# A graph network on one core: the adjacency build's last two column blocks kept as the first layers' ring, and the head's small stages rearranged

## The reference

```python
s = concatenate([src, arange(n)]); d = concatenate([dst, arange(n)]); w = concatenate([edge_weight, ones(n)])
deg = segment_sum(w, d, n); dinv = where(deg > 0, rsqrt(deg), 0.0)
norm = dinv[s] * w * dinv[d]
h = x @ W                                        # once for each layer
out = segment_sum(h[s] * norm[:, None], d, n) + b
```

## Time and profile before

| | us |
|---|---|
| median of three runs | 3757.71 |
| the profiled execution, its time | 3750.24 |
| its span, first to last instruction | 3748.5 |
| search, to the first memset of the build | 50.3 |
| build, to the first load of the degrees | 50.3 to 287.2 |
| degrees, to the first memset of the pair tables | 287.2 to 319.6 |
| pair tables, to the load of x | 319.6 to 354.0 |
| node rows, to the first product of the layers | 354.0 to 377.5 |
| first layers, to the load of the next activation table | 377.5 to 800.3 |

### The profile page before, as it was taken

The page is one execution under the profiler, slowest core; times in us unless marked ns, Lnnn a source line. Parts: engine busy times, 40 slices in busy tenths (PEclk is TensorE's granted clock), DMA queues, the critical chain, the costliest instruction groups (busy, mean ns, idle before and its releaser), DMA issues. The chain is left out here.

```text
span 3748.5 us, 47928 instructions
## 1 busy us (share of the span) xinstructions
PE 3235.0 (86%) x13936; PEld 2084.9 (56%) x13936; DVE 1413.7 (38%) x3323; ACT 1300.0 (35%) x2198; POOL 922.2 (25%) x927
## 2 busy tenths in 40 slices
PE   5872999975999996388888869999999999999994
PEld 3661555544888884277667645555555555555541
DVE  6992100023666665488888840010000000000003
ACT  1440000021555554277777732222222222222223
POOL 2000000005777770077777700000000000000000
PEclk9995999995776776699999979999999999999997
DMA  1443676723333330166566547667667676676740
GB/s 40 187 187 131 289 300 285 302 100 75 77 82 78 82 77 7 55 181 166 161 165 169 158 155 294 281 277 296 277 285 290 272 300 277 278 300 269 292 185 17
DMA packets 172645, 721.48 MB, mean 192 GB/s; under 512 B 43149, under 2 KB 139151, under 8 KB 159724
## 3 DMA queue, kind: packets, MB, share of 16 engines
q1 hardware_dynamic: 128802, 631.24, 42.7%
q0 software_dynamic: 33920, 84.12, 9.2%
q10 hardware_dynamic: 9681, 3.07, 0.3%
HBM read 669.95 MB, written 48.38 MB: 192 GB/s over the span
## 5 line engine op out<-in xcount | busy, mean ns | idle before, releaser
L900 PE MATMUL deep_out_psum<-deep_adjacency,deep_scaled_nodes 125*128 125x450 f32 (+1 forms) x3500 | 1334.6, 537 | 0.0
L900 PEld LDWEIGHTS deep_out_psum<-deep_adjacency,deep_scaled_nodes 125*128 125x128 f32 x3500 | 656.9, 189 | 625.0 <-issue 625.0
L1629 POOL DMA_INDIRECT gate_source_rows_sb<-gate_source_rows,pair_src x416 | 454.0, 1091 | 293.7 <-POOLq L1066 167.2
L1235 POOL DMA_INDIRECT source_rows<-gat_source_rows,pair_src x416 | 420.0, 1010 | 126.8 <-issue 125.0
L900 PE MATMUL gcn_out_psum<-gcn_adjacency,gcn_scaled_nodes 125*128 125x450 f32 (+1 forms) x1050 | 399.1, 539 | 0.0
L1671 PE MATMUL gate_core_psum<-edge_weights,edge_features_t 128*128 128x256 f32 x832 | 263.7, 399 | 46.9 <-ACT edge_features_t L1705 45.5
L900 PEld LDWEIGHTS gcn_out_psum<-gcn_adjacency,gcn_scaled_nodes 125*128 125x128 f32 x1050 | 198.0, 190 | 188.9 <-issue 188.9
L923 ACT ACTIVATE deep_squares<-deep_aggregate,deep_vectors 128x450 f32<-128x450 f32 (+1 forms) x70 | 46.8, 668 | 629.4 <-DVE deep_aggregate L968 629.4
L973 DVE SCALAR_TENSOR_TENSOR deep_normed<-deep_aggregate,deep_vectors,deep_squares 128x450 f32<-128x450 f32 (+1 forms) x70 | 47.9, 685 | 565.5 <-ACT deep_squares L927 565.5
L442 PE MATMUL adjacency_sum<-weighted_cell,source_onehot 128*128 128x150 f32 x1042 | 177.6, 311 | 41.3 <-DVE weighted_cell L418 41.2
L1673 PE MATMUL gate_core_psum<-gate_target_rows,gate_node_onehot_t 125*128 x1248 | 208.5, 275 | 0.0
(11 more groups left out here) (359 smaller groups left out, 4210.5 us busy)
## 6 DMA issues: line engine op xcount, KB each, us to landing
deep_adjacency<-adjacency SPq DMA_DIRECT2D x70, 5625.0 KB, 16.2
gcn_adjacency<-adjacency SPq DMA_DIRECT2D x21, 5625.0 KB, 16.2
adjacency<-adjacency_columns SPq DMA_DIRECT2D x7, 5625.0 KB, 16.9
edge_features<-in_edge_attr_dram SPq DMA_DIRECT2D x416, 64.0 KB
att_node_rows<-pair_dst_rows SPq DMA_DIRECT2D x104, 125.0 KB
gate_node_rows<-pair_dst_rows SPq DMA_DIRECT2D x104, 125.0 KB
source_rows<-gat_source_rows,pair_src POOLq DMA_INDIRECT x416
gate_source_rows_sb<-gate_source_rows,pair_src POOLq DMA_INDIRECT x416
```

The lines of the kernel that those rows point to most:

```text
L900: m = nc.tensor.matmul(op[:, n % 2, 0:cols], h[:, l % 2, s, :], ring[0:T, n % 2, s, 0:cols], start=s == 0, stop=s == NS - 1)
L1235: pool.indirect_dma_start(xj[:, b % HOLD, q, :], None, d["h_r"], bass.IndirectOffsetOnAxis(ap=c["pair_src"][:, b * PQ + q:b * PQ + q + 1], ...
L1629: pool.indirect_dma_start(xj[:, b % 4, q, :], None, d["p_src"], bass.IndirectOffsetOnAxis(ap=c["pair_src"][:, b * PQ + q:b * PQ + q + 1], ...
```

## The change

The build visits the column blocks in the order 2, 3, 4, 5, 6, 0, 1, so blocks 0 and 1 are the last in the staging tile; this tile becomes the first layers' ring, and the layers' first two blocks are read where they were built. All seven blocks are still stored, for the later layers. The tile is allocated from the start, and the search stage uses it as work space.

The node rows are loaded (third in SP's queue) and turned during the search: 25 transposes by TensorE, between the product that finds the rows and the products of the sizes, with copies by ScalarE. The tables of extra blocks (two groups of products and five VectorE instructions) move from the search to the build, after units 6, 13, 14 and 21; block 0's extra passes wait for them. Five small VectorE instructions turn a place in the order into a group's number.

The degree parts go from the stage to 25 rows of SBUF, 25 products with ones sum them into a [125, 25] tile, which is already by nodes; one transpose and a copy give the rows that are stored and then broadcast. The stage waits for the store and no more for the broadcast; the layers' VectorE stream does. The layers' weights are loaded on ScalarE's queue in this stage.

The pair tables' steps stand between the layers' blocks: VectorE's after blocks 0, 2, 4, ... 12 (behind L968), TensorE's after blocks 1, 3, ... 11 (behind the block's last product), ScalarE's loads at the layers' start and its stores after blocks 9 and 11. The stages of pair tables and of node rows are gone, with one reset of the semaphores.

```diff
--- before.py
+++ after.py
...
-        "deg_rows": nc.dram_tensor("degree_part_rows", [NSP, NS, BW], F32).ap(),
...
+HELD = 2
+TURN = (NSP - HELD) * GB
+ORDER = [(b + HELD) % NSP for b in range(NSP)]
...
-def edge_lanes(nc, c, d, x_src, x_dst, x_w):
+def edge_lanes(nc, c, d, x_src, x_dst, x_w, x, columns):
...
+        spare = columns[:, 1, :, :].rearrange("p s c -> p (s c)")
+        el = spare[0:ER, 0:4 * EC].rearrange("p (c w) -> p c w", w=4)
+        xn = columns[0:T, 0, :, 0:D]
...
             sp.dma_start(ei[:, 1, :], x_dst.rearrange("(p c) -> p c", p=ER)).then_inc(s_ld, 16)
             sp.dma_start(ei[:, 0, :], x_src.rearrange("(p c) -> p c", p=ER)).then_inc(s_ls, 16)
+            sp.dma_start(xn, x.rearrange("(s r) f -> r s f", r=T)).then_inc(s_lx, 16)
...
+            for q in range(NXQ):
+                n = min(4, NS - 4 * q)
+                act.wait_ge(s_xt, q + 1)
+                nc.scalar.copy(c["x_t"][:, 4 * q * T:(4 * q + n) * T].rearrange("f (s r) -> f s r", r=T), p_t[:, q % GC, 0:n, 0:T]).then_inc(s_xc, 1)
...
+            pe.wait_ge(s_lx, 16)
+            for s in range(NS):
...
+                t = nc.tensor.transpose(p_t[:, s // 4 % GC, s % 4, 0:T], xn[:, s, :], c["ident"][0:T, 0:T])
...
             pe.wait_ge(s_mask, 1)
             pe.wait_ge(s_sr, 1)
...
-            pe.wait_ge(s_bc, 1)
-            for k in range(GC):
-                m = nc.tensor.matmul(p_g[:, 0:UO], c["ones"][:, :], begun[:, k, :], start=k == 0, stop=k == GC - 1)
-            m.then_inc(s_sp, 1)
-            for k in range(GC):
-                m = nc.tensor.matmul(p_n[0:1, 0:UO], dv[:, k:k + 1], begun[:, k, :], start=k == 0, stop=k == GC - 1)
-            m.then_inc(s_sp, 1)
+            pe.wait_ge(s_xc, NXQ)
...
+            o.link(vec.tensor_scalar(wraps[:, :], place[:, :], float(TURN), -float(NSP * GB), ALU.is_ge, ALU.mult))
+            o.link(vec.scalar_tensor_tensor(group[:, :], place[:, :], float(HELD * GB), wraps[:, :], ALU.add, ALU.add))
+            o.link(vec.tensor_scalar(own[:, 0, :], group[:, :], float(G), None, ALU.mult))
+            vec.tensor_scalar(own[:, 1, :], group[:, :], float(NS * G), None, ALU.mult)
+            o.link(vec.tensor_tensor(node[:, 0, :, :], node[:, 1, :, :], own[:, 0, :].unsqueeze(2).to_broadcast([128, GC, G]), ALU.add))
...
 def build_adjacency(nc, c, d, stage):
...
+        SPREAD_AT, PLACED_AT, FIRST_AT, LISTED_AT = 6, 13, 14, 21
...
+        slot = [(b + NSP - HELD) % 2 for b in range(NSP)]
...
+                if n == PLACED_AT:
+                    dve.wait_ge(s_xs, 1)
+                    vec.tensor_scalar(c["extra_cells"][:, :], xps[:, 0:UO], float(NS * G), float(NS * G * (HELD * GB - 1)), ALU.mult, ALU.add)
+                    vec.tensor_scalar(c["extra_column"][:, :], xps[0:1, 0:UO], float(G), float(G * (HELD * GB - 1)), ALU.mult, ALU.add).then_inc(s_xp, 1)
+                    vec.tensor_scalar(steps[:, :], c["ramp"][0:1, 0:UO], float(EL), float(EL), ALU.mult, ALU.add).then_inc(s_xv, 1)
+                if n == LISTED_AT:
+                    dve.wait_ge(s_xs, 2)
...
+                    vec.tensor_tensor(e0r[:, :], xps[0:1, 0:UO], steps[:, :], ALU.add).then_inc(s_xv, 1)
+                    dve.wait_ge(s_xv, 2)
+                    vec.tensor_scalar(c["extra_first"][:, :], e0r[:, :], float(E), None, ALU.min).then_inc(s_xl, 1)
...
+                if n == SPREAD_AT:
+                    for k in range(GC):
+                        i = nc.tensor.matmul(xps[:, 0:UO], c["group_steps"][:, k, :], c["group_begun"][:, k, :], start=k == 0, stop=k == GC - 1)
+                    i.then_inc(s_xs, 1)
+                if n == FIRST_AT:
+                    pe.wait_ge(s_xp, 1)
+                    for k in range(GC):
+                        i = nc.tensor.matmul(xps[0:1, 0:UO], c["extra_edge_step"][:, k:k + 1], c["group_begun"][:, k, :], start=k == 0, stop=k == GC - 1)
+                    i.then_inc(s_xs, 1)
...
-                sp.dma_start(d["deg_rows"][b:b + 1, :, :], stage[T:T + 1, b % 2, :, :]).then_inc(s_dg, 16)
-                sp.dma_start(d["adj"][b], stage[:, b % 2, :, :]).then_inc(s_st[b % 2], 16)
+                first = ORDER[b] * BW
+                sp.dma_start(c["degree_parts"][0:NS, first:first + BW], stage[T:T + 1, slot[b], :, :]).then_inc(s_dg, 16)
+                sp.dma_start(d["adj"][ORDER[b]], stage[:, slot[b], :, :]).then_inc(s_st[slot[b]], 16)
...
-def degrees(nc, c, d):
+def degrees(nc, c, d, ly):
...
+            for s in range(NS):
+                m = nc.tensor.matmul(p_d[:, s:s + 1], c["degree_parts"][0:NS, s * T:(s + 1) * T], c["ones"][0:NS, 0:1], start=True, stop=True)
+            m.then_inc(s_d, 1)
+            pe.wait_ge(s_n, 1)
+            nc.tensor.transpose(p_r[:, 0:T], c["dinv_n"][:, :], c["ident"][0:T, 0:T]).then_inc(s_t, 1)
...
-            for b in range(NSP):
-                act.dma_start(sums[b * BP:(b + 1) * BP, :, :], d["deg_rows"][b].rearrange("s (x j) -> x s j", j=DJ)).then_inc(s_ld, 16)
+            ly.begin(act, d)
...
+            nc.scalar.copy(c["dinv_rows"][:, :], p_r[:, 0:T]).then_inc(s_c, 1)
+            act.wait_ge(s_c, 1)
+            act.dma_start(d["dinv"].rearrange("(s r) -> s r", r=T), c["dinv_rows"][:, :]).then_inc(s_st, 16)
             act.wait_ge(s_st, 16)
...
-                act.dma_start(c["dinv_n"][:, :], d["dinv"].rearrange("(s r) -> r s", r=T)).then_inc(s_bk, 16)
-            act.dma_start(c["dinv_b"][:, :], d["dinv"].unsqueeze(0).to_broadcast([128, N])).then_inc(s_bk, 16)
-            act.wait_ge(s_bk, 32)
+            act.dma_start(c["dinv_b"][:, :], d["dinv"].unsqueeze(0).to_broadcast([128, N])).then_inc(c["dinv_loaded"], 16)
...
-def edge_path(nc, c, d, x_src, x_dst):
...
+class EdgePath:
...
+    def tensor(self, pe, n):
...
+        if n == 1:
+            pe.wait_ge(self.s_bl, 1)
             for t in range(UTL):
...
+        if n == 3:
+            pe.wait_ge(self.s_ps, 1)
+            nc.tensor.matmul(ps[:, 1, 0:KP], c["ones"][0:NS - 1, :], self.passed[:, :], start=True, stop=True).then_inc(self.s_gr, 1)
+        if n == 5:
+            pe.wait_ge(self.s_pk, 1)
             for t in range(UTL):
+                m = nc.tensor.matmul(ps[:, 2, 0:KP], self.dst_f[:, t, :], self.pick[:, t, :], start=t == 0, stop=t == UTL - 1)
...
+        if n == 7:
+            pe.wait_ge(self.s_dl, 2)
...
+        if n == 9:
+            pe.wait_ge(self.s_tc, 1)
+            pe.wait_ge(self.s_bm, 2)
...
+        if n == 11:
+            pe.wait_ge(self.s_bs, 1)
+            pe.wait_ge(self.s_ba, 8)
...
-def load_transposed(nc, c, tag, x, out, bias=None, then=None):
...
-        self.load(sp, d, 0)
-        self.load(sp, d, 1)
+        for n in range(self.held, 2):
+            self.load(eng, d, n)
...
-def gcn_layers(nc, c, d, ly):
+def gcn_layers(nc, c, d, ly, path=None):
...
+            if ly.held:
+                for k in range(2):
+                    sp.wait_ge(c["adj_stored"][k], 16 * len(range(1 - k, NSP, 2)))
             for n in range(2, len(blocks)):
                 sp.wait_ge(s_bs, n - 1)
                 ly.load(sp, d, n)
...
-                pe.wait_ge(ly.s_a[n % 2], (n // 2 + 1) * 16)
+                if n >= ly.held:
+                    pe.wait_ge(ly.s_a[n % 2], ((n - ly.held) // 2 + 1) * 16)
...
                 m.then_inc(s_bs, 1)
+                if path is not None:
+                    path.tensor(pe, n)
...
+            if ly.held:
+                dve.wait_ge(c["dinv_loaded"], 16)
...
                 vec.tensor_tensor(yk, op[:, n % 2, 0:cols], c["dinv_b"][:, c0:c0 + cols], ALU.mult).then_inc(s_br, 1)
+                if path is not None:
+                    path.vector(dve, n)
...
-        edge_path(nc, c, d, a["src"], a["dst"])
-    c["sems"].end()
...
+        gcn_layers(nc, c, d, ly, EdgePath(nc, c, d, held, a["src"], a["dst"]))
```

477 lines of the change are left out of this document (221 added, 256 removed).

## The result

The changed kernel takes 3698.96 us (median of four executions, 3696.4 to 3705.42) against 3757.88 us for the kernel before (median of four, 3755.4 to 3759.23). The ratio is 0.9847, 95% interval 0.9829 to 0.9864: 58.9 us less, where 71.0 were forecast. The time lies in the forecast's range. The span of the profiled execution went from 3748.5 to 3696.6 us, 51.9 us less, because the profiled execution of before was 7.6 us faster than its median and this one was not.

The account below looks back on a forecast made before the run. VectorE bounds the build, TensorE the first layers, latency chains other head stages. Terms -58.0, -18.1, -7.3, +13.0, +3.0, -3.6 sum to -71.0 us: 3679.2 from the profiled execution, 3686.7 against the median; range 3671 to 3702.

Parts of the forecast that it names:

- Where the time goes: Head: pair-table and node-row stages vanish, -58.0 us; their TensorE work goes into the layers at full clock, +13.0 us.
- Rivals C and D: Layers: C, late ring loads stop TensorE, 3780 us, chance 0.02; D, steps between blocks wait, 3735 us, chance 0.03.
- Degrees and start of the layers: From the degrees' first instruction to the layers' first on TensorE: -58.0 for removed stages and -18.1 for degrees, -76.1 us.
- the 50 products: Degrees: 25 products of two instructions each on TensorE, 6 us at slow clock, then 23 at 0.11, 8.5 us.
- The rest of the chain: Degrees, after the products: PSUM copy 0.45, steps 1.9, transpose and copy 0.8, store 2.0, broadcast's issue and barrier 0.6 us.
- First layers: First layers' stretch: TensorE's share of the tables +13.0 us, start without waiting for the ring -7.3 us; together +5.7.
- Build: Build: five VectorE instructions of up to 0.59 us enter VectorE's full stretch, +3.0 us; TensorE's two groups cost nothing.
- Search: Search: without tables the stage ends 9.0 us earlier, but x delays the edge list by 5.5 us; -3.6 us.
- Rival A: Search: x does not delay the edge list, -9.0 us in place of -3.6; kernel at 3681, chance 0.2.
- rival B: Head: thinner cover; degrees' clock +2.5, no search gain +3.6, layers' start +1.8, tables' places +2; 3697 us, chance 0.2.
- All behind 800 us: Layers, attention and everything behind 800 us keep their code and buffers: no change, 0 us.
- The offset: Whole kernel: profiled execution was 7.5 us below its median, so the forecast was raised from 3679.2 to 3686.7 us.

Follow-up runs that it names:

- warm_tail: The changed kernel with nine products of 418 columns, whose results nobody reads, behind the build's last product; 3692.49 us.
- x_split: The changed kernel with the load of x given as 120 rows and 5 rows instead of 125 at once; 3681.18 us.

## Why the prediction was right, and what was off

**Where the time goes: right.** No stage stands between the degrees and the layers, the tables' products are in the layers at the full clock, and nothing waits for the ring. Rivals C and D are out: TensorE is busy for 421.1 of 422.7 us.

**Degrees and start of the layers.** -74.5 against -76.1. The term that was mis-sized is the 50 products: 8.5 us forecast, with a rise of the clock after 6 us; the whole 10.6 us ran at 0.50. 0.212 us for each is the row of L240 (0.22), as the upper estimate had it. The figure of the page TensorE: Matmul & The Clock Gate of the Trainium skill, section LDWEIGHTS, would have made it 5.2 us. At the full clock of `warm_tail` the first 36 took 3.7 us, 0.10 each, so that P / 1.2 ns is met here at 2.4 GHz and is half the cost at 1.2. The rest of the chain took 5.2 us for 5.8.

**First layers.** +3.8 against +5.7: tables 14.0 (13.0 forecast), start -10.2 (-7.3). The start's size is what is left when the tables are taken out of +3.8; it gained more because the clock was up as soon as the first block's products began (309.5).

**Build.** +3.2 against +3.0. (Half of L258's 6.45 us is 3.2 and not 3.5; TensorE's two groups took 3.67 us each, and the sum had nothing for them.)

**Search.** -1.0 against -3.6. The mechanism was right, as `x_split` shows; two sizes were not, and the working has a slip: a list delayed by 27.3 - 21.2 = 6.1 us lands at 37.2, not 36.6, which is -3.0. The gather started at 38.24 instead of 36.6, since x landed at 31.0 instead of 27.3, and from that gather to the build are 11.1 us instead of 10.0. Rival A is out; of rival B two parts happened, the clock of the degrees' products (+2.1 of its +2.5) and most of the search's lost gain (+2.6 of its +3.6), while the layers' start did not keep its slow stretch.

**All behind 800 us: the one step that failed.** "The layers, attention and all behind 800 us keep their code and buffers: nothing." Same code is not same time: +16.2 us, 15.1 of them in the gated convolution, where each of 416 gathers on GpSimd can lose up to 1.05 us by where it falls in VectorE's loop: the softplus held 71 gathers for 38.0 us before and 88 for 50.9 after, the message product 101 for 18.7 and 101 for 19.6, which is 13.8 of the 13.9 us. Six executions at the ordinary pace, with the loop unchanged, took 570.1 (before), and 585.2, 581.2, 574.2, 576.0 and 575.8 us (the changed kernel and its variants), each 115 to 117 us above its gathers' time. That the gathers' sum sets the stage's length is shown by these and by the run that moved them. That the changed kernel's stage must be longer, or why more of its gathers start within a softplus, is not: the edits that ended at 574 to 576 us left it untouched, and with late landings it was 8.9 us shorter. But only one ordinary execution of before was profiled, itself 7.6 us under its median, and all five of the changed kernel's family were above it. How much of the 15.1 is chance stays open. Between the medians 7.0 us of it are gone: the kernels differ by 58.9, not by 51.9.

**The offset.** Adding 7.5 us to reach the median helped: 3698.96 is 12.0 above the forecast of 3687.0, and would be 19.8 above 3679.2, the forecast from the profiled execution alone.

## What to carry to other kernels

Cut a serial head into stages, price each chain by its rows, and charge every moved step to the engine that is full where it lands: that gave -71.0 for a measured -68.1. Keep a term for untouched stages in which one engine issues without a pause beside two others in a loop; there a shift of phase went with 4 to 15 us in a stage of 570 us. When an instruction of such a stream is late, compare its end with the ends of the others' instructions before it, not only with the one that begins as it falls due. And when a transfer is put in front of another in a queue, look at its partition count: 120 + 5 rows instead of 125 gave back 4.8 us of search.

## What was not expected of the hardware

- In the gated convolution a gather on GpSimd that starts within a VectorE instruction with two inputs in SBUF (0.04 us or more behind its start, 0.135 us or more of it left) ends 0.81 to 0.84 us behind that instruction's end, in all 2315 cases of 14 executions, and takes up to 2.0 us instead of 0.95. With one of the inputs in PSUM (547 cases) it is not held.
- In `warm_tail` TensorE's granted clock fell from 1.00 to 0.50 after 3.7 us of one-column products (125 columns of stationary data each) without a gap, and in the changed kernel it stayed at 0.50 through 10.6 us of them.
- The dense layers took the same on every occasion (1416.4 to 1417.3 us for the deep ones), while attention and gated convolution with their gathers took 1104 us on one and 1555 on another (533.4 + 570.1 and 836.9 + 718.2 for the kernel before, attention from its first scores to its last): a kernel of gathers has to be compared within one occasion.
